# Relational scores and first weights made in the turning stage, and picked attention in five score banks with two turn banks

## The reference, cut to what matters

```python
xr = jnp.einsum('nd,rdf->rnf', x, W)                 # values of 3 relations, W is 3 x 768 x 768
alpha = leaky_relu(oi @ q + oj @ k)                  # scores: 12 (layer 1) or 3 (layer 2) channels
m = segment_max(alpha, dst); e = exp(alpha - m[dst]) # greatest score of each row
out = segment_sum(e / z[dst] * oj, dst)
...
logits = einsum('blhd,bmhd->bhlm', q, kk) / sqrt(dh) # only picked rows are kept: 188 of 1250, 12 heads
probs = softmax(logits); ctx = einsum('bhlm,bmhd->blhd', probs, v)
```

## Time and profile before

| | us |
|---|---|
| median of 3 runs (2974.64 to 2977.48) | 2976.41 |
| the profiled execution's own time | 2970.5 |
| its span | 2968.8 |
| PE busy, DVE busy, ACT busy | 2536.1, 2106.1, 1315.0 |
| relational layer 1: turning, then the scores' block up to the first values | from 1202.2, from 1214.4 |
| relational layer 2: the same | from 1866.6, from 1879.1 |
| picked attention | from 2701.3 |

### The profile page before, as it was taken

How to read it: one execution, slowest core, us unless ns; L and a number is a source line. 1 busy time by engine, 2 the same in 40 slices (tenths; PEclk the granted TensorE clock), 3 DMA queues, 4 the chain that set the end, 5 groups by cost and what they waited for, 6 DMA issues and landing times. The chain is left out here.

```text
span 2968.8 us, 39008 instructions
## 1 busy us (share of the span) xinstructions
PE 2536.1 (85%) x14382; PEld 2118.7 (71%) x14383; DVE 2106.1 (71%) x3030; ACT 1315.0 (44%) x1649; POOL 310.4 (10%) x166
## 2 busy tenths in 40 slices
PE   6877894888856994799699999699999979998888
PEld 3556892232323994699699999599888769896668
DVE  6775899999974555699689988660567687136555
ACT  1573225989831000222578776221565563222431
POOL 0000000000003794000000000331000000000013
PEclk9997656999976997899899999899999999999989
DMA  2467542611104554455646643452634362311012
GB/s 69 131 174 180 150 150 67 237 52 35 35 33 178 189 197 158 154 180 160 201 121 181 170 118 90 150 171 81 187 122 129 102 194 70 85 54 59 1 41 80
DMA packets 174702, 366.47 MB, mean 123 GB/s; under 512 B 24871, under 2 KB 103541, under 8 KB 174034
## 3 DMA queue, kind: packets, MB, share of 16 engines
q1 hardware_dynamic: 122024, 274.54, 30.9%
q10 hardware_dynamic: 49312, 73.97, 7.4%
q0 software_dynamic: 3200, 15.73, 1.5%
HBM read 281.06 MB, written 83.12 MB: 123 GB/s over the span
## 5 line engine op out<-in xcount | busy, mean ns | idle before, releaser
L1649 PE MATMUL gat_acc<-far_u,gat_ft 125*65 125x512 f32 x720 | 286.3, 538 | 58.1 <-DVE far_u L1717 57.6
L2246 PE MATMUL rg_out<-rg_w,rg_hT 128*125 128x256 f32 (+1 forms) x900 | 276.6, 307 | 8.0 <-POOL rg_w L1185 8.0
L2247 PE MATMUL rg_out<-rg_w,rg_hT 128*125 128x256 f32 (+1 forms) x900 | 275.5, 306 | 0.0
L2248 PE MATMUL rg_out<-rg_w,rg_hT 128*125 128x256 f32 (+1 forms) x900 | 275.3, 306 | 0.0
L1649 PEld LDWEIGHTS gat_acc<-far_u,gat_ft 125*65 125x65 f32 x720 | 93.7, 142 | 246.9 <-issue 153.6
L2246 PE MATMUL rg2a_acc<-rg2a_value_part,rg2a_wts_part 125*125 125x512 f32 x600 | 204.8, 341 | 14.8 <-DVE rg2a_wts_part L1958 11.4
L2247 PE MATMUL rg2a_acc<-rg2a_value_part,rg2a_wts_part 125*125 125x512 f32 x600 | 205.5, 342 | 0.0
L2248 PE MATMUL rg2a_acc<-rg2a_value_part,rg2a_wts_part 125*125 125x512 f32 x600 | 203.8, 340 | 0.0
L1684 ACT ACTIVATE far_u<-gat_rows,gat_ks 125x1250 f32<-125x1250 f32 x118 | 156.7, 1328 | 41.8 <-PE gat_acc L1649 32.7
L2246 PEld LDWEIGHTS rg_out<-rg_w,rg_hT 128*125 128x125 f32 x900 | 169.1, 188 | 8.2 <-issue 8.0
L1697 DVE TENSOR_TENSOR far_u<-far_u,gat_lowb 125x1250 f32<-125x1250 f32 x120 | 174.4, 1454 | 0.4 <-PEq L711 0.4
(11 more groups left out here) (531 smaller groups left out, 6369.3 us busy)
## 6 DMA issues: line engine op xcount, KB each, us to landing
rg2a_values<-values_dram SPq DMA_DIRECT2D x89, 384.0 KB, 3.2
rg1a_counts<-counts_dram SPq DMA_DIRECT2D x26, 820.3 KB
rg_mask<-far_dram SPq DMA_DIRECT2D x60, 312.5 KB, 3.2
moe_raw<-in_L_ffn_w SPq DMA_DIRECT2D x16, 1152.0 KB, 6.9
relw_chunk<-in_L_gnn_W ACTq DMA_DIRECT2D x36, 384.0 KB, 3.1
gat_rows<-rows_dram SPq DMA_DIRECT2D x10, 1250.0 KB, 5.7
sorted_dram<-gat_zeros SPq DMA_DIRECT2D x30, 384.0 KB, 8.9
values_dram<-rg_stage ACTq DMA_DIRECT2D x90, 128.0 KB, 2.9
```

The source lines that it names most:

```text
L1649: last = pe.matmul(acc[h % 2][0:WIDTH, b, 0:c1 - c0], ft[:, t, h, :], wts[i % HB][:, c0:c1], start=(t == 0), stop=(t == NT - 1))
L2246: pe.matmul(out, still[0], moving[0], start=first, stop=False)
L2247: pe.matmul(out, still[0], moving[1], start=False, stop=False)
L2248: return pe.matmul(out, still[1], moving[0], start=False, stop=final)
```

## The change

1. The scores are made in `turn_in_parts`. The PSUM tile of the scores (three banks) now lives outside both blocks, so the turns have two pairs of banks in place of three. PE makes group 0 of the scores after the turn of tile 5, group 1 after tile 9, and then group 2. DVE splits the score weights at the block's start.
2. The first weights are loaded at the start of `turn_in_parts` by ACT (`load_first`: one piece and the bias in layer 1, two halves and the bias in layer 2). ACT makes their high part after tile 7, DVE their low part after its last tile; POOL starts with weights 1 in layer 2. In layer 1 the load of piece 1 is issued by ACT at the start of `greatest`.
3. `LOW_AT` is two passes earlier; `keep_late` comes before the copy of its step in place of after it.
4. ROOM is 80 in place of 40.
5. The picked attention holds both units' scores side by side in five banks. The middle bank is shared, and the second unit's part of it is written after a wait for the first unit's. The turned pieces get two banks, one for each half; four buffers hold probabilities in place of three. PE turns both halves in a row and then makes a whole context. DVE takes both maxima before it takes a context; both exponentials wait for both maxima, and ACT runs them together after the two copies of an even unit.

```diff
-    ROOM = 40
+    ROOM = 80
-LOW_AT = tuple(range(8, 120, 14))[0:8]
+LOW_AT = tuple(range(6, 120, 14))[0:8]
...
     # RelationValues
+    def load_first(self, act):
         self.load_piece(act, 0)
         act.dma_start(self.bias[:, :], rows_of(self.b, P, 0, D)).then_inc(self.bias_in, 16)
-        self.make_high(act, 0)
+    def load(self, act):
+        act.wait_ge(self.low, 1)
+        self.load_piece(act, 1)
...
+            if n == steps - 4:
+                self.keep_late(act)
             act.wait_ge(self.made, n + 1)
...
     # turn_in_parts: PE
+            def scores(j):
+                t0, t1 = GROUPS[j]
+                if j == 0:
+                    pe.wait_ge(ends_set, 2)
+                    pe.wait_ge(weights_split, 2)
+                pe.wait_ge(low_out, 2 * t1)
+                out = scores_ps[:, j, 0:(t1 - t0) * (TP + 1)]
+                for c in range(KC):
+                    last = three(pe, out, [x[:, c, :] for x in weight_parts], ..., c == 0, c == KC - 1)
+                last.then_inc(scores_made, 1)
             for t in range(NT):
-                if t >= 3:
-                    pe.wait_ge(low_out, 2 * (t - 2))
-                turn_tile(pe, g, banks[t % 3], h, t, turned)
+                if t >= 2:
+                    pe.wait_ge(low_out, 2 * (t - 1))
+                turn_tile(pe, g, banks[t % 2], h, t, turned)
+                if t in (5, 9):
+                    scores(t // 4 - 1)
+            scores(2)
     # ACT
+            values.load_first(act)
...
+                if t == 7:
+                    values.make_high(act, 0)
     # DVE
+            dve.tensor_copy(weight_parts[0][:, :, :], flat).then_inc(weights_split, 1)
...
+            values.make_low(dve, 0)
...
     # attend_picked
-    PB = 3
+    PB = 4
-        score_ps = [s.ps(f"att_score{i}", [128, 3, 512]) for i in range(2)]
-        turn_ps = s.ps("att_turn", [TP, 512])
+        all_ps = s.ps("att_score", [128, 5, 512])
+        turn_ps = [s.ps(f"att_turn{i}", [TP, 512]) for i in range(2)]
+        pieces = [((1024, N), (1536 - N, 2048 - N)), ((0, 512), (2048 - N, N)), ((512, 1024), (0, 1536 - N))]
...
-                cut = 7 if i % 2 == 0 else NT
                 turn(i, 0)
+                turn(i, 1)
                 if i:
-                    context(i - 1, 0, cut)
-                turn(i, 1)
-                if i and cut < NT:
-                    context(i - 1, cut, NT)
+                    context(i - 1)
...
                 first_half(a)
+                first_half(a + 1)
                 if a >= 4:
                     take_context(a - 3)
-                first_half(a + 1)
...
-                act.wait_ge(topped, i + 1)
+                act.wait_ge(topped, i // 2 * 2 + 2)
...
-                    if i % 2 == 0 and i + 2 < len(units):
-                        exponential(i + 2 + half)
+                if i % 2 == 0 and i + 2 < len(units):
+                    exponential(i + 2)
+                    exponential(i + 3)
```

## The result

The changed kernel takes 2940.1 us in the median of four runs (2933.9 to 2941.7), the kernel before 2976.9 in four runs on the same chip: a ratio of 0.9882 with a 95% interval of [0.9862, 0.9902], some 35 us less. The forecast was 22.7 less.

The account below looks back on a forecast made before the run. It took DVE's passes to bound layer 1, PE layer 2, and PE's work plus waits the picked attention. Terms -7.8 + 1.6 - 3.9 + 2.4 - 15 = -22.7 on median 2976.41 gave 2953.7 us, range 2941 to 2971.

Parts of the forecast that it names:

- PE sets the pace at 8.90: Picked attention: PE's 8.90 us of work bounds a pair, taken as 9.05 in place of 10.34; 15 us gained.
- The last pair: Picked attention: the last pair loses its own waits, some 2 us gained.
- The later start: Picked attention: the first exponential waits for the second maximum, 1.6 us late once.
- the ring: Picked attention: scores, maxima, exponentials, next scores as the other bound on a pair, 8.7 us.
- Rival A: Picked attention: score pieces go one after the other, 11.0 us a pair; total about 2974 us; chance 0.06.
- Layer 2: Relational layer 2: values start earlier without waiting for POOL's low part; 7.8 us gained, bounds 4 and 10.
- both mechanisms: Layer 1: row write held up behind masks and counts, 1.6 us lost; `keep_late` before its copy, 3.9 gained.
- one of the three things named as making me wrong: Pair over 9.5 us, layer 1's fourth pass over 4 us later in its layer, or PE waiting in layer 2's values.
- Barriers: Between blocks: five clearing barriers for three, 1.2 us each; 2.4 us lost, bounds 1.6 and 3.3.
- Rival B: Relational layers: clock stays low in turning and scores, 8 us a layer; total 2970 us; chance 0.12.
- Rival D: Picked attention: denser work is granted less clock; with 35% of PE work at 1.2 GHz about 2991 us; chance 0.05.
- Rival C: Layer 1's row write isn't held up and the attention reaches 8.7 us a pair; total 2944 us; chance 0.17.

Follow-up runs that it names:

- experiment 6: Changed kernel with PE's old order in the picked attention: a unit's two turns apart, an even unit's context in two parts; 2938.9 us, 0.9881.
- experiment 7: Changed kernel with DVE again taking a context between the two maxima of a pair; 2958.2 us, 0.9942.
- experiment 8: Changed kernel with one bank for turned pieces again, the other unused; 2983.4 us, 1.0029.
- experiment 11: The changed kernel run once more, unchanged; 2937.3 us, 0.9884.
- experiments 1 and 2: First: kernel before with only the new picked attention, 2946.8 us, 0.9901. Second: changed kernel with the old picked attention, 2963.3 us, 0.9953.
- experiment 4: Changed kernel with SP in layer 1 issuing one mask, the row write and four row loads before other masks and counts; 2931.6 us, 0.9844.

## Why the prediction was right in direction and too small

**The term that failed is the picked attention: "PE sets the pace at 8.90", 15 us gained; it was 24.4.** I read PE's busy 8.90 of a pair as work that can't shrink. It shrank to 8.34 with the same 72 matmuls. Turning five pieces costs 0.78 by itself before (2752.47), ten in a row 1.33 now; PE's old order costs 0.47 a pair with no wait of PE (experiment 6). So most of the difference is PE changing from one kind of matmul to another, and putting equal ones together removes it. Nine intervals at 2.01 give 18.1, where I had counted eleven at 1.29. The second interval gives 3.1, with a granted clock of 0.73 in place of 0.53. The last pair gives 4.5 where I put 2 (from the last scores to the first matmul of the bias 19.38, now 14.91), with a clock of 1.00 in place of 0.93. The later start costs 1.3 where I put 1.6. That makes the 24.4. How much of the second and the last pair is clock alone was not separated. The other bound, the ring, I had at 8.7 with 3.1 for the two exponentials; back to back they take 2.66, and the ring too comes to 8.3.

**What carries it.** DVE's order (experiment 7, 21.4) and the two turn banks (experiment 8, 45.8) are each needed: without one of them nearly all or more than all of the gain goes. These are not shares, for each was taken out while the other stayed. In experiment 8 waits of PE are 2.46 of the 3.8 us that a pair takes more; the rest is longer busy time, with less clock granted beside it. The fourth buffer for probabilities and ACT's new order were not taken back alone.

**Score pieces.** Rival A fell: six unequal pieces take 2.34 us. The Trainium skill, TensorE: Matmul & The Clock Gate, section "The mechanism", has matmuls start and end in program order across row groups, which I had worked through to an estimate of 2.1 to 2.4. The 2.34 agrees with it, but it would be the same if each half of the array went on by itself; only going in step, at 2.8, and going one after the other are ruled out.

**Layer 2 was right**: 7.9 against 7.8, by the steps given: no wait for POOL, first value 2.5 us after `greatest` starts (forecast 2.7), turning block 24.2.

**Layer 1: both mechanisms were right, one size was wrong.** The write was held up, 8.8 us (forecast 7 or more), but done 12.2 us after the block's start where I had 10.5, and the rows took 11.2 to the fourth pass where I had 8.4 to 10.3. Fourth pass 4.5 later in its layer, against 1.6: beyond my bound of 4, and one of the three things named as making me wrong. Both came from an average rate over a longer stretch; why these loads went below it I didn't test. So the layer lost 1.9 where I had it gain 2.3: 4.5 at the fourth pass and 1.0 in the passes behind it, less the 3.6 that `keep_late` gave back (forecast 3.9).

**Barriers** 2.7 in the trace against 2.4.

**The clock.** Rival B fell: granted 1.00 from 6 us into the block to its end. The rule of the Trainium skill that I cited for it (TensorE: Matmul & The Clock Gate, section "A second HAM failure mode: psum-queue depth-cycling") is not borne out by two pairs of banks here. Rival D fell: PE is busy for all of 60 us in the attention at 1.00.

**Rival C** had half of it: the pair went below its 8.7, while the write was held up.

**That the total stayed at the range's edge is luck.** The attention gave 9.4 more than forecast, 8.8 came from stages whose code didn't change, and layer 1 gave 4.2 less: without that last error the time would lie below 2941 by the ratio too.

**What stays open.** The changed stages sum to 7.9 - 1.9 - 2.7 + 24.4, or 27.8 before rounding, while the profiled executions differ by 36.6 and the medians by 36.9 (35 by the ratio). The remaining 8.8 lie in code that wasn't changed. Such stages vary among kernels with the same code in them: the graph attention ends at 839 to 847 us, the first relational attention takes 415.9 to 421.3, the feed-forward 87.5 to 90.8. The feed-forward differs by 2.4 between two executions of the changed kernel, the end of the graph attention only by 0.2 (experiment 11). Nor do the parts add up: experiments 1 and 2 timed 29.5 and 14.0 us less, 43.5 together, more than the whole. I tried nothing that would tell placement in memory from chance here.

**The better version** is experiment 4: 0.9844 against 0.9882 [0.9862, 0.9902] and 0.9884 [0.9868, 0.99] for the changed kernel, and the layer's trace shows 7.7 of these some 11 us.

## What to carry to other kernels

An engine's busy time in a stage isn't a floor: what stands between unlike instructions counts as busy, and grouping like ones removes it. When work is moved out of the block that a bulk load was hiding behind, look at the first small write on the same queue; it now pays for what was issued ahead of it. Here reordering the queue gave 7.7 us, where the layer had lost 1.9 without it. And when one bound of a stage is lowered, work out the next bound from durations back to back, not from rows in which they were apart.

## What the runs showed of the hardware that I had not expected

- Turns in five take 0.78 us, ten in a row 1.33, and a pair with three more changes of kind takes 0.47 longer.
- The clock rose to 1.00 within the first 6 us of the turning block and stayed to its end, with PE busy 14.98 of the next 16.80 us; behind the block, after 2.35 us without work for PE, it was 0.50. In experiment 8, with PE busy 47.68 of 60, it fell to 0.92.
- A write of a few rows took 8.8, 3.7 or 2.0 us, by what stood ahead of it on the queue and on ACT's (four masks, counts and a piece; one mask and a piece; one mask).
